# Column attention's norm and its first products in one program, with pair 0 handled ahead of the others

## What is computed

```
x = x + attn_a(layernorm(x))        # linear attention
x = x + ffn(layernorm(x))           # two layers: windowed attention, then gated products (gelu)
x = x + attn_b(layernorm(x))        # column attention
x = x + ffn(layernorm(x))           # the same two layers again
return x

def attn_b(X, Wq, bq, Wk, bk, Wv, bv, Wo, bo):
    Q, K, V = X @ Wq + bq, X @ Wk + bk, X @ Wv + bv
    Q, K, V = (t.reshape(N, 16, 256, 8) for t in (Q, K, V))   # a plain reshape, no transpose
    scores = einsum('neax,nebx->neab', Q * scale, K * scale)
    A = softmax(scores, axis=2)                               # over a, the row index
    Out = einsum('neab,neax->neax', A, V).reshape(N, 256, 128)
    return Out @ Wo + bo
```

## Time and profile before

| what | value |
|---|---|
| median of 3 runs | 1855.08 us (1852.59 to 1858.78) |
| the profiled execution | 1854.08 us, of which its span, from first to last instruction, is 1852.3 us |
| granted PE clock, mean | 0.971 of full speed |
| PE busy | 1699.6 us, 92% of the span |
| DVE busy | 1377.2 us, 74% |
| ACT busy | 1311.5 us, 71% |
| POOL busy | 1119.9 us, 60% |
| layer 1's last residual begins | 848.82 us |
| the norm block begins | 849.84 us |
| the column block's first product | 872.10 us |
| first scores | 900.53 us |
| the next ffn layer begins | 1161.3 us |

### The profile page before, as it was taken

One profiled execution on the slowest core, in us unless ns is written; L12 is line 12 of the kernel. 1 busy time (PEld: TensorE's weight loads), 2 busy tenths in 40 slices (PEclk: granted clock), 3 DMA queues, 4 the chain that ended last, 5 costly groups with the idle time before them and its releaser, 6 DMA issues. The chain is left out here.

```text
span 1852.3 us, 43550 instructions
## 1 busy us (share of the span) xinstructions
PE 1699.6 (92%) x15560; PEld 1105.6 (60%) x15560; DVE 1377.2 (74%) x2369; ACT 1311.5 (71%) x4480; POOL 1119.9 (60%) x1006
## 2 busy tenths in 40 slices
PE   7997899998989999997599999799999899999999
PEld 4664577775557777554244444467776556777655
DVE  4553999993689999455488888599996488999645
ACT  4444688887348888734499999588888537888753
POOL 3554899993379999601222220699997178999730
PEclk8999999999999999999799999899999999999999
DMA  2002111103011110200765652211102102110111
GB/s 64 2 2 58 26 32 25 25 19 81 15 35 24 30 28 21 53 1 16 112 107 92 107 92 35 66 30 24 31 20 57 49 1 53 25 30 19 42 23 46
DMA packets 72830, 74.81 MB, mean 40 GB/s; under 512 B 18644, under 2 KB 56744, under 8 KB 70568
## 3 DMA queue, kind: packets, MB, share of 16 engines
q1 hardware_dynamic: 72616, 72.03, 19.0%
HBM read 27.99 MB, written 10.49 MB: 21 GB/s over the span
## 5 line engine op out<-in xcount | busy, mean ns | idle before, releaser
L498 POOL TENSOR_TENSOR rsum<-pa,pb 128x512 f32<-128x512 f32 x256 | 325.5, 1291 | 57.5 <-DVE pa L416 40.4
L877 ACT ACTIVATE ffn_prob<-sc,ffn_nmax 128x128 f32<-128x128 f32 x928 | 327.5, 388 | 5.0 <-DVE ffn_nmax L798 5.0
L964 POOL TENSOR_TENSOR ffn_prob<-ffn_prob,ffn_rden 128x512 f32<-128x512 f32 x256 | 265.6, 1059 | 70.0 <-DVE ffn_rden L808 69.8
L507 POOL TENSOR_TENSOR rsum<-rsum,ffn_rnt 128x512 f32<-128x512 f32 x256 | 261.8, 1044 | 10.9 <-ACT ffn_rnt L899 8.6
L877 ACT ACTIVATION_READ_ACCUMULATOR ffn_prob<-sc,ffn_nmax 128x1 f32 x928 | 210.5, 227 | 0.0
L426 DVE TENSOR_TENSOR pb<-proj,ffn_tab 128x512 f32<-128x512 f32 x236 | 161.4, 684 | 59.3 <-ACT rn L468 58.7
L406 PE MATMUL pt<-ident,rsum 128*128 128x128 f32 x960 | 154.6, 284 | 13.5 <-POOL rsum L507 10.7
L798 DVE TENSOR_REDUCE ffn_nmax<-sc 128x4 f32<-128x512 f32 x232 | 148.5, 681 | 13.4 <-PE sc L692 10.4
L406 PEld LDWEIGHTS pt<-ident,rsum 128*128 128x128 f32 x960 | 101.0, 141 | 95.3 <-ACT ffn_ptb L885 70.4
L1819 ACT ACTIVATE column_E<-proj,column_nm 128x256 f32<-128x256 f32 x256 | 123.8, 512 | 44.1 <-DVE column_nm L1743 43.6
L435 DVE TENSOR_REDUCE ffn_ss<-rn 128x16 f32<-128x1024 f32 x128 | 154.5, 1207 | 0.0
(11 more groups left out here) (280 smaller groups left out, 4381.8 us busy)
## 6 DMA issues: line engine op xcount, KB each, us to landing
ffn_v<-ffn_v SPq DMA_DIRECT2D x128, 128.0 KB, 2.3
column_ks<-qk_parts SPq DMA_DIRECT2D x64, 128.0 KB
rn<-Y SPq DMA_DIRECT2D x32, 128.0 KB, 2.4
qk_parts<-column_hi SPq DMA_DIRECT2D x64, 64.0 KB, 2.0
qk_parts<-column_lo SPq DMA_DIRECT2D x64, 64.0 KB, 1.9
column_qs<-qk_parts SPq DMA_DIRECT2D x32, 128.0 KB
column_qs<-qk_parts SPq DMA_DIRECT2D x64, 64.0 KB
rn<-Y SPq DMA_DIRECT2D x32, 127.5 KB, 2.4
```

The lines of the kernel that those rows point to most:

```text
L498: pool.tensor_tensor(K.sm[:, r, w], K.m1[:, r, w], K.m2[:, r, w], ALU.add).then_inc(S.f_sum, 1)
L507: pool.tensor_tensor(heads(K.sm[:, r, w]), heads(K.sm[:, r, w]), K.rnt[:, r, w * HEADS:(w + 1) * HEADS].unsqueeze(2).broadcast_to([P, HEAD ...
L877: ins = act.activation(K.prob[:, r, e, k], score_banks(i)[e][:, tokens(k)], ACT.Exp, bias=K.nmax[:, r, e, k:k + 1], accum_out=K.den[:, r, ...
L964: pool.tensor_tensor(K.prob[:, r, e], K.prob[:, r, e], K.rden[:, r, e].unsqueeze(2).broadcast_to([P, 4, P]), ALU.mult).then_inc(S.f_pn, 1)
```

## The change

The norm block is gone, and its work stands in two other places:

- **In the gated products of layer 1** (`feeds`): the whole norm of pair 0 up to the division by the deviation. PE gets the centring at step 6 and the averaging at step 8, ACT the square at step 7; after the 24th gelu ACT loads the table set that has logarithm and exponential, and makes both; DVE makes `column_normal` ahead of the last residual. SP loads the weights at the start of this stage, in 2 transfers in place of 24, into a tile (`K.rn`) that is free by then. The host turns the columns of Wq and Wk and lays weights and biases side by side.
- **In the column block**: pair 0's split, its q and k and their split in parts come first; the norms of pairs 1 to 7 and the products of pair 1 are interleaved behind. POOL splits the weights, clears the tiles, and makes the low parts of the norms 1 to 7; ACT makes the high parts of pair 0's q and k, DVE their low parts.
- **Transfers**: the 16 writes of a pair are two groups of 8 (`write_sequence`), each with a semaphore of its own, and a load waits for its own sequence's 8 writes alone. Sequence 0 is written and its load issued ahead of the writes of sequence 1. Inside a group each write waits for its own part.
- **First scores** wait for all products of pairs 0 and 1 and for all norms too, since they use the same banks.
- ACT's exponentials of this block run with the table set `natural_log_exp_and_others` in place of `exp_and_others`.

```
 gated_programs:
+    feeds = last and not final
+        if feeds:                                   # sync, at the start
+            load_column_weights(sp, K)
+            if feeds and x == 6:                    # tensor
+                pe.wait_ge(S.ff_y, PAIRS * n + 1)
+                column_centre(pe, K, 0)
+            if feeds and x == 8:
+                column_variance(pe, K, 0)
+            if feeds and x == 7:                    # scalar
+                column_square(act, K, 0)
+        if feeds:                                   # scalar, after the last gelu
+            act.preload_act_table_set("natural_log_exp_and_others")
+            column_inverse_root(act, K, 0)
+        if feeds:                                   # vector
+            column_normal(dve, K, 0)
         residual(PAIRS - 1)
...
 column_attention_block, sync:
-            write(0)
+            write_sequence(0)
             load(0)
+            write_sequence(1)
             load(1)
-            write(1)
+            write_sequence(2)
+            write_sequence(3)
             for i in range(PAIRS - 1):
                 load(2 * i + 2)
                 if i + 2 < PAIRS:
-                    write(i + 2)
+                    write_sequence(2 * i + 4)
+                    write_sequence(2 * i + 5)
                 load(2 * i + 3)
 gpsimd:
-            parts(0)
+            split_column_weights(pool, K, B)
+            pool.memset(B.ks[:].bitcast(F32), 0.0).then_inc(S.b_zero, 1)
+            pool.memset(B.rd[:], 0.0).then_inc(S.b_zero, 1)
+            for p in range(1, PAIRS - 2):
+                column_low(pool, K, p)
+            reorder(0)
+            for p in range(PAIRS - 2, PAIRS):
+                column_low(pool, K, p)
             parts(1)
-            reorder(0)
             reorder(1)
 scores, q == 0:
-                        pe.wait_ge(S.b_full, 3)
+                        pe.wait_ge(S.b_full, 6)
+                        pe.wait_ge(S.ln_nrm, ENTRY + PAIRS)
 scalar:
-            act.preload_act_table_set("exp_and_others")
+            act.preload_act_table_set("natural_log_exp_and_others")
+            column_square(act, K, 1)
+            column_square(act, K, 2)
+            for j in range(2):
+                act.wait_ge(S.b_full, j + 1)
+                act.copy(B.hi[:, j], B.full[:, j]).then_inc(S.b_hi, 1)
+            for p in range(1, PAIRS):
+                column_inverse_root(act, K, p)
+                if p + 2 < PAIRS:
+                    column_square(act, K, p + 2)
```

More of the change, by code:

```diff
@@ L1561, in split_column_weights @@
[L1561 to L1572 removed]
+    sp.dma_start(K.cw, d["c_column"]).then_inc(S.b_in, 16)
@@ new lines, in load_column_weights, with split_column_weights, column_centre @@
+    sp.dma_start(K.spread, d["c_spread"]).then_inc(S.b_in, 16)
+def split_column_weights(pool, K, B):
+    S = K.s
+    pool.wait_ge(S.b_in, 32)
+    pool.tensor_copy(B.w_hi[:], B.w[:, 0:3]).then_inc(S.b_whi, 1)
+    pool.wait_ge(S.b_whi, 1)
+    pool.tensor_tensor(B.w_lo[:], B.w[:, 0:3], B.w_hi[:].bitcast(F32), ALU.subtract).then_inc(S.b_wlo, 1)
+def column_centre(pe, K, p):
+    S = K.s
+    if p >= 4:
+        pe.wait_ge(S.ln_nrm, ENTRY + p - 3)
+    pe.matmul(column_cent(K, p)[:], K.cent_w[:], K.X[:, pair(p)], start=True, stop=True).then_inc(S.ln_cent, 1)
@@ new lines, in column_variance, with column_square, column_inverse_root @@
+def column_variance(pe, K, p):
+    S = K.s
+    pe.wait_ge(S.ln_sq, ENTRY + p + 1)
+    if p >= 2:
+        pe.wait_ge(S.ln_log, ENTRY + p - 1)
+    pe.matmul(column_var(K, p)[:], K.mean_w[:], K.lnq[:, p % 2], start=True, stop=True).then_inc(S.ln_var, 1)
+def column_square(act, K, p):
+    S = K.s
+    act.wait_ge(S.ln_cent, ENTRY + p + 1)
+    if p >= 2:
+        act.wait_ge(S.ln_var, ENTRY + p - 1)
+    act.activation(K.lnq[:, p % 2], column_cent(K, p)[:], ACT.Square).then_inc(S.ln_sq, 1)
+def column_inverse_root(act, K, p):
+    S = K.s
+    act.wait_ge(S.ln_var, ENTRY + p + 1)
+    act.activation(K.lnl[:, p % 2], column_var(K, p)[:], ACT.Ln, bias=K.eps[:]).then_inc(S.ln_log, 1)
+    act.wait_ge(S.ln_log, ENTRY + p + 1)
+    if p >= 2:
+        act.wait_ge(S.ln_nrm, ENTRY + p - 1)
+    act.activation(K.lnr[:, p % 2], K.lnl[:, p % 2], ACT.Exp, scale=-0.5).then_inc(S.ln_rstd, 1)
@@ new lines, in column_normal, with column_high, column_low @@
+def column_normal(dve, K, p):
+    S = K.s
+    dve.wait_ge(S.ln_rstd, ENTRY + p + 1)
+    if p >= 2:
+        dve.wait_ge(S.ln_lo, PAIRS + p - 1)
+    dve.tensor_tensor(K.lnf[:, p % 2], column_cent(K, p)[:], K.lnr[:, p % 2], ALU.mult).then_inc(S.ln_nrm, 1)
+def column_high(dve, K, p):
+    S = K.s
+    dve.wait_ge(S.ln_nrm, ENTRY + p + 1)
+    dve.tensor_copy(K.HI[:, pair(p)], K.lnf[:, p % 2]).then_inc(S.ln_hi, 1)
+def column_low(engine, K, p):
+    S = K.s
+    engine.wait_ge(S.ln_hi, PAIRS + p + 1)
+    engine.tensor_tensor(K.LO[:, pair(p)], K.lnf[:, p % 2], K.HI[:, pair(p)].bitcast(F32), ALU.subtract).then_inc(S.ln_lo, 1)
@@ L1701, in project @@
                 pe.matmul(K.pt[0][:, 0:SEQ], B.w[:, 3], B.o[:], start=True, stop=True).then_inc(S.b_wo, 1)
-            for g in range(2):
-                for j in range(3):
-                    product(g, j)
+            column_centre(pe, K, 1)
+            column_centre(pe, K, 2)
+            product(0, 0)
+            product(0, 1)
+            column_variance(pe, K, 1)
+            column_centre(pe, K, 3)
+            column_variance(pe, K, 2)
+            product(0, 2)
+            column_centre(pe, K, 4)
+            column_variance(pe, K, 3)
+            column_centre(pe, K, 5)
+            column_variance(pe, K, 4)
+            product(1, 0)
+            column_centre(pe, K, 6)
+            column_variance(pe, K, 5)
+            product(1, 1)
+            column_centre(pe, K, 7)
+            column_variance(pe, K, 6)
+            product(1, 2)
+            column_variance(pe, K, 7)
             for q in range(SEQS):
@@ L1929, in __init__ @@
         self.b_hi = new("b_hi")
-        self.b_out0 = new("b_out0")
-        self.b_out1 = new("b_out1")
+        self.b_bs = new("b_bs")
+        self.b_zero = new("b_zero")
+        self.b_wlo = new("b_wlo")
+        self.b_out = [[new(f"b_out{k}{s}") for s in range(2)] for k in range(2)]
         self.b_ld0 = new("b_ld0")
```

180 lines of the change are left out of this document (65 added, 115 removed).

## The result

The changed kernel takes **1829.24 us** (median of 4 runs, 1828.47 to 1830.51) against 1854.84 of the kernel before on the same chip (4 runs, 1852.59 to 1858.78): 0.9861 of it, with a 95% interval of 0.9849 to 0.9873. The same kernel, measured twice more beside the experiments, gave 0.9885 (0.9863 to 0.9908) and 0.9867 (0.9846 to 0.9888). Forecast: 1831, a gain of 23.8.

What follows compares the result with a forecast made beforehand. The uncovered chain from the norm block's start to the first scores was taken as the bound: 26.8 us saved there, less 1.7 and 1.3 paid ahead, gives 23.8 gained and 1831 us forecast, range 1826.5 to 1838.

Steps and rivals of the forecast that it cites:

- The bound: Column block's start to first scores: 50.66 us, one chain of norm, weights, products, split, writes, read and reorder.
- The gated stage, +1.7: Gated products: one centring and one averaging added on PE cost 1.7 us; at least 0 if idle time absorbs them.
- The stage's end, +1.3: After the last gelu: table load, logarithm, exponential and multiplication end the stage 1.3 us later, between 0.6 and 2.7.
- the 2.7 with a drain: Gated stage's end: cost of 2.7 us instead of 1.3 if the table switch also takes a 1.38 us drain.
- Block start to first product, 1.75: Column block's start: first product after 1.75 us in place of 22.23, set by PE's two centrings; saves 20.5.
- First product to first read, 7.2: Column block: products, parts and eight writes take 7.2 us before the read, in place of 13.57; saves 6.3.
- Read and reorder, 14.9: First read and POOL's reorder stay at 12.90 and 1.96 us; a 12.2 us read would gain 0.7 more.
- First scores at 23.8: Column block: first scores 23.8 us after its start in place of 50.66, 26.8 less.
- Norms under cover, end by 19: Norms of pairs 1 to 7 run during writes and read, ending by about 19 us, some 5 to spare.
- Sequence 1 in time: Sequence 1's reorder ends at 39 us, its scores due at 38.7: just in time or late by up to 1.
- The rival of a late sequence 1: Sequence 1's reorder ends at 41.5 us, gain only 20 to 21; chance 0.25, with late sequence 2 or similar losses.
- The other table set: Column block's 512 exponentials slower: 46 ns each cancels the gain, 60 gives 1862 us; chance 0.04, shared with recurring waits.

Runs made afterwards that it cites:

- the second trace: The changed kernel measured again with nothing changed, as a control: 1832.32 us against 1854.57 of the kernel before.
- The added wait: Changed kernel, but DVE makes pair 0's low part only after POOL has split the weights: 1832.61 us against 1853.16 of the kernel before, single run.
- the late clearing: Against the kernel of "all together", POOL clears its large tile only after DVE has made pair 0's low part: 1829.67 us, ratio 0.9867 to the kernel before.
- no part ahead: Changed kernel, but pair 0's norm stands at the column block's start, not in the gated products: 1833.94 us, ratio 0.989 to the kernel before.
- all together: Changed kernel plus merged writes, even reads, last residual ahead of pair 0's multiplication, and weights' split on POOL in the gated stage: 1830.73 us, ratio 0.9872.
- the residual first: Changed kernel, but DVE makes the gated products' last residual ahead of pair 0's multiplication: 1827.39 us, ratio 0.9867 to the kernel before.

## Why the prediction was right

**The bound.** Right. One chain from the block's start to the first scores had no cover; taking 26.4 off it (50.66 to 24.3) took 21.4 off the touched stretch and some 24 off the time. What was put ahead of it was paid.

**The gated stage, +1.7.** Right. The two steps of the gated loop that have norm work in them took 3.12 us from one gelu to the next in place of 2.25, +1.74 together. G differs by 0.8 among the three traces for another reason, the clock at the stage's start: where it falls and rises as it did before (in the second trace), G is 3.02 longer, just the 1.7 and 1.3 of the forecast.

**The stage's end, +1.3.** Right: 5.01 us from the last gelu's start to the block's start, against 3.76. The table load starts 0.02 behind the gelu's end and the next step 0.02 behind the load, so the 2.7 with a drain falls. There was 0.64 to save, by the order of DVE's last two steps.

**Block start to first product, 1.75.** This term was mis-sized: 2.42, in all three traces. I took PE's two centrings for the latest and cost DVE's three steps at 1.3, with POOL's split beside them for nothing. Those steps took 0.50, 0.41 and 1.37. The added wait and the late clearing show the cause: with POOL apart they take 0.17, 0.42 and 0.69. The first product then comes at 1.43, with no idle time of PE ahead of it, so the two centrings alone would have let it begin 0.3 earlier than forecast. The Trainium skill (page "SBUF — State Buffer", section "Who interferes with whom") says that VectorE and GpSimd share a pair of SBUF ports, locked for a whole instruction, which casts and tensor_scalar on VectorE can take, and that a tensor_tensor with two SBUF inputs contends with a GpSimd instruction that reads and not with one that only writes. DVE's 3.65 and 3.83 beside a clearing of 3.52 agree, and so does the low part's 0.69 beside the same clearing. The low part began at 853.75 and POOL's subtraction ended at 854.58; a full stop until then and 0.69 of work would be 1.52, the row has 1.37, so here too it stood still for nearly the whole of the overlap.

**First product to first read, 7.2.** 7.36, 8.03 and 7.36: right, including the 0.45 per issue and the 1.2 of landing. The forecast assumed PE's higher clock at the first products. That held in two of the three traces; in the one with 8.03 it was the lower one, which costs the 0.7. So that condition was not met each time, and a little of the 13.57 of before, whose window stood at 0.75, was the clock too.

**Read and reorder, 14.9.** 12.39 and 1.99, 14.4: 0.5 less. The read has writes behind it and not another read; with the read back behind it, it took 12.93. I named 12.2 as the other end and took the wrong one.

**First scores at 23.8.** 24.2, 24.7 and 24.0. The late low part and the shorter read nearly cancel.

**Norms under cover, end by 19.** Right: the last multiplication ends at 872.25, 19.4 behind the start. In the kernel with no part ahead the cover held too.

**Sequence 1 in time.** Right: the reorder was over 38.0 behind the start (forecast 39), and its scores came 15.05 behind the first, 14.85 before. The rival of a late sequence 1 falls. The margin is 1.2 us, from the reorder's end at 890.89 to the scores at 892.06: a little more in the queue would have decided it.

**The other table set.** No effect. The changed kernel's exponentials (columns: minimum, median, maximum of one, in ns, then the first and the last start) against 464/494/665 in the earlier trace rows, 1 ns more in the minimum:

```profile
L1875 ACT ACTIVATE column_E<-proj,column_nm x256: 465/494/663, 878.5 to 1130.3; 128x256 f32<-128x256 f32 x128
```

**What wasn't in the sum.** T grew by 1.1 to 1.7. PE's timeline at the column stage's end, and a window of it, of the kernel before:

```profile
1158.18 1.13 PE L1696 MATMUL pt<-column_z,column_sel 128*128 128x256 f32 x4 [0.85 <-DVE column_z L1765]
...
1158.00:1160.00 2.00, 1.30 (x5) 0.85 (x6) 0.55 (x2) 0.00 (x0) 0.00 (x0) 1.00 0.00 0
```

And of the changed kernel:

```profile
1134.91 2.07 PE L1711 MATMUL pt<-column_z,rn 128*128 128x256 f32 x4 [0.85 <-DVE column_z L1797]
...
1136.00:1138.00 2.00, 1.48 (x4) 0.76 (x3) 0.42 (x1) 0.00 (x0) 0.00 (x0) 0.50 0.00 0
```

The same four products take 2.07 in place of 1.13: PE's granted clock is at 0.50, the 1.2 GHz level, where before it stayed at 1.00, the 2.4 GHz level. PE did the same light work ahead in both. This is not a mark of the change, though. In the second trace of the changed kernel, the one with no part ahead and "all together" the four products still took 1.13, and the clock fell just behind them; in the one with the residual first it did not fall at all:

```profile
1138.00:1143.00 5.00, 2.79 (x10) 1.46 (x9) 1.66 (x4) 0.80 (x1) 0.80 (x1) 1.00 0.00 0
```

From those products' start to the end of T it is 4.66, 3.71 and 4.66 us in the three traces, 3.19 before and 3.19 with the residual first. So 0.5 to 1.5 of T's growth is the clock at the tail. The remaining 0.2 to 0.6 goes with how long the clock stays low behind the first scores, 8.6 to 10.6 us in place of 8. Why it falls in one trace and not in another stays open.

**Where it doesn't close.** The stretch gained 21.4 in the mean of three traces, and the medians 24. The remaining 2.6 lie outside the stretch that the change touches: in these three traces the part behind it is 3.7 to 4.6 shorter than in the one trace of before, but its wander over all the kernels, 5 us, covers that. PE's clock was low there for some 33 us before and 25 in these three, which would fit, but the kernel with the residual first has 26 us and the longest rest of all, 691.2. The cause of the 2.6 stays open. That 23.8 came so near 24 is therefore partly luck: its own terms, as measured and with T, come to 21.4.

## What to carry to other kernels

When all engines wait for one first transfer, look for the smallest piece of work that it needs, do that first, and put the rest under the transfer: most of the gain here came with that order, some 4 us of it from splitting the writes, and only 1.0 to 1.4 us from starting the piece in the stage before. Cost casts and tensor_scalar steps within SBUF on VectorE as if they shared a port with whatever GpSimd does beside them, and two-operand steps so beside a GpSimd step that reads, whatever their sizes: a clearing that could begin earlier, once the work ahead of it was gone, held the first product back by 2.4 us. And look at a transfer's outermost dimension: on a read that the whole kernel waits for, ten transfers, some of 8 rows, against eight of 16 was 1.6 us. Before calling a difference of 1 us yours, compare traces with the same clock at the same places: here it moved the first scores by 0.7 and a stage by over 1.

## What the runs showed of the hardware

- A DVE step of 128x2 that takes 0.17 us took 3.65 beside a POOL MEMSET of 3.52, which reads nothing; the cast behind it was drawn out too, 3.83 in place of 0.42. POOL's clearing took 3.52 there and 3.52 behind DVE's steps.
- Of two two-operand steps on DVE and POOL beside each other, only the one that began later was drawn out: 1.37 in place of 0.69 on DVE, while POOL's took 1.13, and 1.13 again when DVE stood still but for its cast at the beginning; with DVE wholly still it took 0.99.
- Not every DVE step is drawn out beside POOL: its two steps that take the first products out of PSUM took 1.41 together beside the clearing (856.31 in the first trace, the clearing from 854.52 to 858.04), as they did with the clearing past (1.41 with no part ahead), and a two-operand step within SBUF took its 0.69 beside it.
- In traces of the same kernel PE's granted clock behind the first product was 1.00, 0.56 and 1.00, with the same idle time of 2.35 us and the same work ahead of it in the block.
- Half as many writes of twice the size landed 0.25 us later behind the last issue (1.47 against 1.22).
- Between profiles of the same code, stretches of 690 to 790 us differ by 5 to 6 us.
